# Router folded into the out-projection and the first stage's projection

## The reference

```python
x = x + attn(layernorm(x))
x = x + ffn(layernorm(x))

# attn: a state space model along the sequence, then a gated unit
u = (xn @ in_W.T + in_b) per channel
y = gelu(causal_conv(u, k(log_dt, C, A)) + u * D_skip)
a, g = split(glu_W @ y + glu_b)
return (a * sigmoid(g)) @ out_W.T + out_b + xn

# ffn: 14 routed experts, the 2 best of each token, and 2 shared experts
gates = softmax(xf @ router_w)
top_v, top_i = top_k(gates, 2)
masked = top_v normalised to a sum of 1
routed_out = sum over e of masked[e] * (silu(rmsnorm_e(xf) @ W1[e]) @ W2[e])
return routed_out + shared expert 0 + shared expert 1
```

## Time and profile before

| | |
|---|---|
| median of 3 runs | 320.05 us (315.87 to 323.77) |
| profiled execution | 317.75 us |
| its span on the core | 316.0 us |
| PE busy | 256.7 us (81%) |
| VectorE busy | 230.1 us (73%) |
| GpSimd busy | 165.2 us (52%) |
| ScalarE busy | 163.2 us (52%) |

### The profile page before, as it was taken

How to read it: one execution, slowest core, us unless ns; L and a number is a source line. 1 busy time by engine, 2 the same in 40 slices (tenths; PEclk the granted TensorE clock), 3 DMA queues, 4 the chain that set the end, 5 groups by cost and what they waited for, 6 DMA issues and landing times.

```text
span 316.0 us, 8652 instructions
## 1 busy us (share of the span) xinstructions
PE 256.7 (81%) x2812; PEld 234.3 (74%) x2812; DVE 230.1 (73%) x842; ACT 163.2 (52%) x318; POOL 165.2 (52%) x218
## 2 busy tenths in 40 slices
PE   1794376584499687999999889998999999999970
PEld 0794366573387455898888779998999999899970
DVE  6999997969952288877778576746868888886251
ACT  0477538459675475666775363534344444444320
POOL 2489400000048002777777777711747777777771
PEclk9999587789789999999999799999999999999995
DMA  5793009669999960111111145343555666664331
GB/s 124 206 389 146 0 23 263 175 173 285 304 308 291 311 203 11 50 52 52 52 59 53 51 125 161 123 130 107 156 150 138 188 166 196 185 193 134 104 84 50
DMA packets 72725, 47.17 MB, mean 149 GB/s; under 512 B 6241, under 2 KB 70129, under 8 KB 72177
## 3 DMA queue, kind: packets, MB, share of 16 engines
q1 hardware_dynamic: 66000, 37.07, 40.0%
q0 software_dynamic: 4096, 8.40, 9.2%
q10 hardware_dynamic: 2592, 1.26, 1.6%
HBM read 28.66 MB, written 18.06 MB: 148 GB/s over the span
## 4 chain that ended last, share of the span: by engine, by line
PE 51%; DVE 17%; issue 9%; DMA 8%; POOL 5%; ACT 4%; DVEq 3%; SPq 2%; POOLq 1%; ACTq 0%
PE bank L1692 9%; PE bank L1703 8%; POOL area L651 5%; PE bank L1608 5%; PE bank L1595 4%; PE bank L1435 3%; PE bank L1497 3%; PE bank L1683 2%; DMA area<-kp_dram 2%; DVE stats L703 2%; DMA kp_dram<-xnT 2%; PE bank L1424 2%; PE bank L1543 2%; PE bank L1535 2%; DVE u L748 2%
## 5 line engine op out<-in xcount | busy, mean ns | idle before, releaser
L632 POOL DMA_INDIRECT xs_dram<-area x64 | 64.2, 1004 | 41.1 <-issue 40.2
L651 POOL DMA_INDIRECT area<-y_dram,u x64 | 67.1, 1048 | 35.1 <-issue 21.6
L1692 PE MATMUL bank<-xn,v 128*128 128x128 f32 x320 | 43.0, 277 | 0.4 <-DVE x_sb L947 0.3
L1013 DVE COPY v<-v 128x512 f32 x84 | 34.3, 450 | 9.5 <-issue 9.2
L1703 PE MATMUL bank<-v,xn 128*128 128x128 f32 x312 | 41.2, 275 | 0.0
L1692 PEld LDWEIGHTS bank<-xn,v 128*128 128x128 f32 x320 | 38.8, 192 | 1.8 <-DVE x_sb L947 0.5
L1703 PEld LDWEIGHTS bank<-v,xn 128*128 128x128 f32 x312 | 38.0, 192 | 0.0
L1360 ACT ACTIVATE xn<-bank 128x512 f32<-128x512 f32 x40 | 23.9, 597 | 21.6 <-PE bank L1692 21.0
L1355 ACT COPY xn<-bank 128x256 f32<-128x256 f32 x41 | 15.2, 372 | 26.4 <-PE bank L1683 26.4
L1072 DVE COPY u<-bank 128x256 f32<-128x256 f32 x39 | 16.4, 420 | 10.3 <-PE bank L1703 10.0
L1092 DVE SCALAR_TENSOR_TENSOR x_sb<-area,u,x_sb 128x128 f32<-128x128 f32 x64 | 18.3, 347 | 4.1 <-DMA area<-y_dram,u 2.7
(11 more groups left out here) (319 smaller groups left out, 603.6 us busy)
## 6 DMA issues: line engine op xcount, KB each, us to landing
area<-kp_dram SPq DMA_DIRECT2D x12, 512.0 KB, 6.6
y_dram<-xinit SPq DMA_DIRECT2D x1, 4992.0 KB, 19.4
area<-xs_dram SPq DMA_DIRECT2D x78, 64.0 KB, 1.9
y_dram<-u SPq DMA_DIRECT2D x39, 128.0 KB
x_sb<-in_L_attn_x SPq DMA_DIRECT2D x4, 512.0 KB, 8.2
area<-ab_dram SPq DMA_DIRECT2D x2, 1024.0 KB, 5.9
xn<-ab_dram SPq DMA_DIRECT2D x2, 1024.0 KB, 11.1
xn<-kp_dram SPq DMA_DIRECT2D x4, 512.0 KB, 6.7
```

What stands on the lines that cost most here:

```text
L632: pool.indirect_dma_start(out=xs_dram.ap(), out_offset=bass.IndirectOffsetOnAxis(ap=pos[:, k, i:i + 1], axis=0), in_=hx[:, i, :], in_offse ...
L651: pool.indirect_dma_start(out=yl[:, k, i, :], out_offset=None, in_=y_dram.ap(), in_offset=bass.IndirectOffsetOnAxis(ap=slot_of[:, k, i:i + ...
L1013: v.tensor_copy(wc[:, z % STEP], v1_flat.rearrange("p (w m) -> p w m", w=2)[:, :, bass.ds(r, HID)]).then_inc(wc_ready, 1)
L1692: last = mm(bank[2 + p % 2][:, HID * j + P * c:HID * j + P * c + P], wc[:, (2 * p + j) % STEP, 1, P * c:P * c + P], xsT[:, p % 3, P * j:P ...
```

## The change

The router's logits are linear in x2, so they are made of two parts. The part from the layer's input, `lx`, is found in the first stage: `project_routes(i)` multiplies the same `xnT` by `rw`, 14 columns for each tile, and one more matmul with `exch` puts the tokens back in order. ACT writes the result to DRAM (`lx_dram`) and loads it again later; DVE then applies the layernorm's factor and the bias's share (`outb_rw`, from `outb_col`). The part from the out-projection comes from 14 more columns of its weights, `w_out`, which hold the out-projection's weights times `rw` (a matmul of `wnat` and `rw` in the first stage). The mean of `rw` is taken off at the start, by a matmul with `even` and a subtraction on DVE ahead of `ln_stats`.

So `project_out` has 142 columns a tile and its PSUM tile holds x2's addend and the logits' addend; `turn_x2`, `route`, ACT's copy of the turned x2 and their semaphores are gone. `chunk_step(c)` does norm and routes of the same chunk, with eight steps instead of nine; the logits' scale by the norm is applied after the last step, for all chunks at once. The counts go to other PSUM banks, the exponentials stand three shared units later, `shared_out` waits for the addition of the shared units before it, and the gathers of a chunk share one semaphore, but for the last chunk. The load of `rw` and one of `out_b` as a column stand ahead of the other biases on ACT's queue, and PE waits for the three loads counted by `rms_in` before `turn_x(0)`. `project_in(7)` waits for the first `evict_u`, since its PSUM bank is used twice now, where it waited for `rstdr`.

```diff
+        outs = ctx.enter_context(nc.psum_tensor("outs", [P, 1024], F32))
+        bank += [outs[:, 0:512], outs[:, 512:1024]]
+        bank += [ctx.enter_context(nc.psum_tensor(f"bank{i}", [P, 512], F32))[:] for i in range(6, 8)]
+        WIDE = D + E
+        outs_by = outs[:].rearrange("p (b m) -> p b m", b=2)[:, :, 0:2 * WIDE].rearrange("p b (t m) -> p b t m", t=2)
...
+        w_all = sb("w_all", [P, E + 4 * P + E])
+        rw, w_out = w_all[:, 0:E], w_all[:, E + 3 * P:E + 4 * P + E]
+        wT = w_all[:, E:E + 4 * P].rearrange("p (c m) -> p c m", c=4)
+        lraw, lturned = [st[:, 0].rearrange("p x c -> p (x c)")[:, NT * E * i:NT * E * i + NT * E] for i in range(2)]
+        lx = area[:, 4096:4096 + NT * E]
...
+            dve.wait_ge(rwm_ps, 1)
+            v.tensor_tensor(rw, rw, bank[5][:, 0:E], ALU.subtract).then_inc(rwc_ready, 1)
...
+            dve.wait_ge(lx_in, 16)
+            v.tensor_tensor(lx_by, lx_by, rs1p[:].unsqueeze(2).broadcast_to([P, NT, E]), ALU.mult)
+            v.drain()
+            v.tensor_tensor(lx_by, lx_by, outb_rw[:].unsqueeze(1).broadcast_to([P, NT, E]), ALU.add)
...
+                k = slice(TILES * c, TILES * c + TILES)
+                src, y0, tmp, root = vars2[:, c], root0[:, c], roott[:, c], roots[:, c]
+                dve.wait_ge(o_ps, c + 1)
+                by_pair = lgs[:, k].rearrange("p (b t) e -> p b t e", b=2)
+                v.tensor_tensor(by_pair, outs_by[:, :, :, D:], lx_by[:, k].rearrange("p (b t) e -> p b t e", b=2), ALU.add)
+                x2 = x_sb[:, k].rearrange("p (b t) d -> p b t d", b=2)
+                v.tensor_tensor(x2, outs_by[:, :, :, 0:D], x2, ALU.add).then_inc(x2_ready, 1)
+                v.drain()
+                for i in range(TILES * c, TILES * c + TILES):
...
+                v.tensor_copy(seen[:, :, 0], upto[:, :, TILES]).then_inc(m_ready, 1)
+                v.tensor_tensor(tmp, tmp, y0, ALU.mult)
+                if c + 1 < CH:
+                    glu(c + 1)
...
+                dve.wait_ge(rank_ps, c + 1)
+                slot = bank[1][:, 0:TILES * E].rearrange("p (i e) -> p i e", e=E).unsqueeze(1).broadcast_to([P, 2, TILES, E])
+                v.tensor_tensor(sel, oh, slot, ALU.mult).then_inc(rank_used, 1)
...
+            act.dma_start(rw, router_w).then_inc(rms_in, 16)
+            act.dma_start(outb_col[:], out_b.rearrange("(p o) -> p o", o=1), allow_slow_non_contiguous=True).then_inc(b_in, 16)
...
-            a.copy(rstdr[:], bank[1][:, 0:NT]).then_inc(rev_ready, 1)
+            a.copy(rstdr[:], bank[7][:, NT * E:NT * E + NT]).then_inc(rev_ready, 1)
+            a.copy(lraw, bank[7][:, 0:NT * E]).then_inc(lraw_ready, 1)
             magnitude(2)
+            act.wait_ge(lx_ps, 1)
+            a.copy(lturned, bank[7][:, 0:NT * E]).then_inc(lx_ready, 1)
+            act.wait_ge(lx_ready, 1)
+            act.dma_start(lx_dram.ap(), lturned).then_inc(lx_out, 16)
             magnitude(3)
...
+            act.wait_ge(lx_out, 16)
+            act.dma_start(lx, lx_dram.ap()).then_inc(lx_in, 16)
...
+            pe.wait_ge(rms_in, 48)
+            mm(bank[5][:, 0:E], even, rw, start=True, stop=True).then_inc(rwm_ps, 1)
...
                 if i == 7:
-                    pe.wait_ge(rev_ready, 1)
+                    pe.wait_ge(u_ready, 1)
...
+            def project_routes(i):
+                pe.wait_ge(xnT_ready, i + 1)
+                for c in range(4 * i, 4 * i + 4):
+                    mm(bank[7][:, E * c:E * c + E], xnT[:, i % 2, P * (c % 4):P * (c % 4) + P], rw, start=True, stop=True)
...
             for i in range(8):
                 if i < 7:
                     turn_x(i + 1)
+                if i == 0:
+                    pe.wait_ge(rwc_ready, 1)
+                    pe.wait_ge(b_in, 64)
+                    mm(bank[5][:, E:2 * E], outb_col[:].broadcast_to([P, P]), rw, start=True, stop=True)
+                    mm(bank[5][:, 2 * E:3 * E], wnat[:, 3, :], rw, start=True, stop=True).then_inc(wr_ps, 1)
+                project_routes(i)
                 if i == 7:
-                    pe.wait_ge(xnT_ready, 8)
                     pe.wait_ge(scaled, 1)
-                    mm(bank[1][:, 0:NT], exch[:], rstd[:], start=True, stop=True).then_inc(rev_ps, 1)
+                    mm(bank[7][:, NT * E:NT * E + NT], exch[:], rstd[:], start=True, stop=True).then_inc(rev_ps, 1)
                 project_in(i)
 
+            pe.wait_ge(lraw_ready, 1)
+            mm(bank[7][:, 0:NT * E], exch[:], lraw, start=True, stop=True).then_inc(lx_ps, 1)
...
-                    last = mm(bank[4][:, P * q:P * q + P], aT[:, c % 2, P * q:P * q + P], wT[:, 3, :], start=True, stop=True)
+                    last = mm(outs_by[:, q // 2, q % 2], aT[:, c % 2, P * q:P * q + P], w_out, start=True, stop=True)
                 last.then_inc(o_ps, 1)
...
-                turn_x2(i)
...
-                route(i)
-                if i >= 1:
-                    count_routes(i - 1)
+                count_routes(i)
```

More of the change, by code:

```diff
@@ new lines, in chunk_step @@
+                v.drain()
+                if c == CH - 1:
+                    v.tensor_copy(ptab[0:1], after[0:1]).then_inc(ptab_ready, 1)
+                with nc.allow_low_precision(reason="the sums are whole numbers"):
+                    v.tensor_reduce(pos[:, :, k], sel, AX.X, ALU.add).then_inc(pos_ready, 1)
+                v.tensor_tensor(tmp, tmp, y0, ALU.mult)
+                v.drain()
+                v.tensor_scalar(root, tmp, 0.375, -1.25, ALU.mult, ALU.add)
+                v.drain()
@@ L1173, in _ @@
                 evict_xnT(i)
+            act.wait_ge(wr_ps, 1)
+            a.activation(w_out[:, D:], bank[5][:, 2 * E:3 * E], ACT.Copy, scale=0.5)
+            a.copy(outb_rw[:], bank[5][:, E:2 * E]).then_inc(wr_ready, 1)
             act.wait_ge(ab_ready, 1)
@@ L1518, in _ @@
             pe.wait_ge(iota_ready, 1)
-            mm(bank[1][:, 0:E], ones, rw[:], start=True, stop=True).then_inc(rwm_ps, 1)
             def turn_y(c):
```

236 lines of the change are left out of this document (95 added, 141 removed).

## The result

The changed kernel takes 326.15 us (median of five runs, 325.09 to 328.6); the kernel before, run beside it, 316.38 (five runs, 315.87 to 323.77). The ratio is 1.0269, with a 95% interval of 1.0214 to 1.0323: slower, by 9.8 us. The profiled execution took 328.6, the slowest of the five, with a span of 326.7 where it was 316.0, so the two profiles differ by 10.7.

The account below looks back on a forecast made before the run. Taken as bounds: the first stage's start of the products, the woven PE step, and when scatters and expert loop begin. 317.75 + 10.9 - 6.3 = 322.35 profiled, plus 2.3 for the median: 324.6, range 318.5 to 330.

Parts of the forecast that it names:

- within 2%: Whole kernel: time stays within about 2% of the kernel before, 313.7 to 326.4; chance .60, slower .35, faster .05.
- (a): First stage: PE waits for all of `rms_in` ahead of `turn_x(0)`, moving it from 9.88 to 13.6, +3.7 (+1.8 to +4.8).
- (b): First stage on PE: two more fold matmuls, four passes at .236, cost .9.
- (c): First stage on PE: `project_routes`, eight times four matmuls of 14 columns, all on the path, 6.7 (6.4 to 7.1).
- the rival that they overlap: First stage: route matmuls go at the narrowest ones' pace, .94 instead of 6.7, median 318.9; chance .10.
- (d): First stage: ACT's copy of the reversed `rstd` moves to 37.8 and `evict_u(0)` with it, +7.8.
- (e): First stage: new chain from `evict_u(0)` over `project_in(7)`, `lx` matmul, copy, store and sines; products at 46.3, +10.9.
- The shift is carried whole: Between products and first residual: states, tables and Hankel loads follow the products, so the +10.9 passes on unchanged.
- The lx load: Before the odd evictions: ACT's load of `lx`, issued near 92, lands by 99, 6.6 after issue; cost 0.
- The GLU stage: GLU stage: PE's step shortens from 9.18 to 8.0, scatters start 3.0 sooner, first expert matmul 6.3 sooner (-6.6 to -2.5).
- The rival on the step that doesn't shorten: GLU stage: PE waits for same-step masks, steps stay near 9.2, gain only 2.5, median 328.4; chance .13.
- the late `lx`: Odd evictions: the `lx` load lands at 103, last eviction done at 107, +3.9, 328.5; chance .10.

Follow-up runs that it names:

- e1: Changed kernel with ACT's copy of the turned logits and its store moved behind the sines of groups 0 and 1; ratio 1.0106 to the kernel before.
- e4: Changed kernel with 112 empty instructions put ahead of PE's first wait, which were not in the program; ratio 1.0279 to the kernel before.
- e4b: Changed kernel with 42 small matmuls (84 passes) ahead of PE's first wait for the weights; ratio 1.0166 to the kernel before.
- e5: Kernel before with only 32 matmuls of 14 columns (64 passes) added ahead of the projections of the eight rounds; median 324.94 beside 319.02.
- e10: Kernel before with 42 narrow matmuls at PE's start and nothing of the change; ratio 1.0112 to the kernel before.
- e11: e7 plus 42 small matmuls at PE's start and DVE's two operations on `lx` moved behind the last evictions; ratio .9925 to the kernel before.
- e8: Changed kernel with PE's removed work (four turns, four 14-column matmuls, on constants) put back into each GLU step; ratio 1.0401 to the kernel before.
- e6: Changed kernel with all route matmuls behind the reversed deviations, `rw` awaited behind the second turn, logits' copies and store behind the sines; ratio 1.0103.
- e7: e6 with PE's gaps ahead of the routes cut (magnitudes later, fold in rounds 1 and 3) and the last projection in the routes' middle; ratio .9985.

## Why the prediction was right or wrong

The time of 326.15 lies in the range of 318.5 to 330, and 1.5 over the forecast; but the forecast's likeliest case was "within 2%", and the kernel is slower by more than that. The difference was sized at half: +4.6 worked out, +9.8 measured (+10.7 between the profiles). That the time still came out within 1.5 is in part luck: the sum started from a median of three runs, 320.05, and with five runs the median of before is 316.38, 3.7 lower. The points in their order:

**(a) The wait for `rms_in`**: +3.7 forecast, +2.7 measured; the loads landed at 12.1. In its range.

**(b), (c) Fold and routes**: .9 and 6.7 forecast. The fold took .7 (16.12 to 16.84). The routes take .81 to .93 a round behind the first, 6.9 in all, so the rival that they overlap is out. Together with (a) the reversing matmul came at 35.95, where the sum had 37.2: right to 1.3.

**(d), (e) The chain over `lx`**: `evict_u` at 36.65 (forecast 37.8), the products at 47.02 (46.3), so +11.8 (+10.9 was forecast, by 35.32). The mechanism held piece by piece. The pieces differ: the last projection and the `lx` matmul take 1.84 and 1.55 to the next step instead of .89 and .8, because PE idles 1.68 ahead of them and goes on at a lower granted clock (.70 over 36 to 40 us, the first row below), while the store costs ACT .36 instead of .67. e1 shows the part that ACT's order has: 4.4, where 3.1 had been set apart.

The row of stretches of the change, 36 to 40 and 78 to 82 us (granted clock third from the end):

```profile
36.00:40.00 4.00, 2.32 (x12) 2.24 (x13) 3.35 (x13) 1.67 (x3) 0.00 (x0) 0.70 0.00 0
78.00:82.00 4.00, 4.00 (x59) 3.69 (x59) 3.29 (x7) 1.76 (x3) 0.00 (x0) 0.57 0.46 138
```

**"The shift is carried whole"**: this step failed; the sum had nothing for it. 4.4 us were lost between products and first residual. Of these 2.4 come up to the last write to `kp_dram`, and e4, the same program, has them too. PE's code load behind 853 passes fell into the states of the last group, where PE is waited for (3.18), and PE went on from it at a clock of .57 (78 to 82 us; the turns at 78.50 take 1.93 for eight passes, before it was 1.99 for sixteen). So this group took 4.7 longer, and 2.3 had been gained ahead of it, where the kernel before has its gaps of 1.31, 2.32 and 2.92. e4b, e5 and e10 show it from three sides: moved within the change, brought into the kernel before by the routes alone, and by matmuls that do nothing. The gaps were in the trace of before; I had read them as a part of the stage, not as something that moves when instructions are added ahead of it.

Of the other 2.0, .7 is the wait for the evictions behind `lx` (e11). About 1.0 came with the Hankel loads, where a landing took 8.55 instead of 6.66; but e4, with the same program, took 14.8 from the last write to the last Hankel product, the change 17.3 and the kernel before 16.2, so that this is not shown to belong to the change. What made these loads longer was not tried.

**The lx load**: it landed 5.9 after its issue (forecast 6.6). DVE waited 7.70 for it, which was named as a sign of being wrong, but the landing itself held up little. Its two operations took 2.7 each instead of .6, which the sum had covered, and the cover held all but .7 of it.

**The GLU stage**: 8.0 for a step forecast; 7.4 to 8.1 measured, set by DVE. Step 7 starts 54.4 behind step 0 (55.2 forecast), the first scatter 10.0 (10.4), the first expert matmul 79.75 (80.0). Against the earlier trace rows that is -6.6, and -5.6 is left at the last gather; -6.3 was forecast. (The 14 columns in `project_out`, put at .08, are .12 by the ratio of columns; nothing hung on it.) The rival on the step that doesn't shorten is out, as is the late `lx`. In the profile of e8 PE's work carries 1.3 of it; by the timed runs it may be more.

So 10.9 - 6.3 became 11.8 + 4.4 - 5.6 = 10.6: two terms right within a microsecond, and a third that the sum had at zero.

## What to carry to other kernels

A stage's gaps without a releaser can be code loads, and these stand at fixed counts of instructions: an edit that adds instructions early moves every later stage against them, so count the passes up to each gap and see into which group it will fall. Look for the packet of the instruction queue first: the 1.54 ahead of the first turn of y reads "issue" too, and was a wait for DVE. Hiding work in an engine's idle time needs a look at what stands behind it in the same queue: e6 and e7 put 64 passes where PE waited, and they took twice as long there. And before an instruction that waits is put among others, as `lx`'s copy among ACT's sines, ask what is queued behind it: moving it was worth 4.4 us up to the products.

## What the runs showed of the hardware

PE's code loads: from the products to the last Hankel product, its gaps without a releaser (.2 to 4.5 us) stood behind 345, 472, 600, 726, 853, 980 or 1107 passes in all profiles (one or two off). Each ended 1.1 to 1.6 us behind the end of a packet of .02 MB on the instruction queue; the longer gaps hold the whole packet. A pass is a matmul and a weight load, so 127 passes are 254 instructions. The Trainium skill, "Advanced Engine Details and Errata", section "ISA Cache", has a line of 16 KB, 256 instructions; the traces agree with that. Not every line shows a gap: 726 and 853 passed without one in the kernel before. The gap ahead of the first turn of y is of another kind: it stands in that line behind 1360 passes in the change and behind 1444 in e4b, with no packet in the 4 us ahead of it.

PE's clock: 64 passes of 14-column matmuls ran at a granted clock of .50 for 12 us and more (e6), and in e7 it fell from 1.00 to .50 in the first 32 of them, while the same matmuls between projections and turns ran at 1.00 (the change). At a run's start PE goes at half pace up to the first rise in the trace's list of clock changes, though the rows read 1.00 there: 14.57 before, 17.14 in the change, 26.96 in e4. Between the last two, the same program, it moved the first eviction by 4.4 (36.65 and 41.03) and the first residual not at all (126.47 and 126.51).
